# The first layer of a two-layer block, with its output products in three f32r terms and its order of work rewritten

## The reference

```
xn  = layernorm(x)
h   = rms_norm(xn) * norm_w
gate, hs = gelu(h @ fc_gate_w.T + b), h @ fc_w.T + b
r, i     = sigmoid(h @ fc_r_w.T + b), sigmoid(h @ fc_i_w.T + b)
a   = exp(-8 * softplus(alpha) * r)
s   = sqrt(1 - a*a) * hs * i
o_t = a_t * o_(t-1) + s_t                     # along each sequence
hs2 = o * gate + xn
h2  = rms_norm(hs2) * norm2_w
attn = ((h2 @ mlp_fc_w.T + b) * gelu(h2 @ mlp_gate_w.T + b)) @ out_w.T + out_b + hs2
ffn  = bitlinear(relu(bitlinear(xn, w_fc) + gate * (xn @ v.T @ fast_b.T @ u.T))**2, w_proj)
x1   = x + attn + ffn
```

## Time and profile before

| what | value |
|---|---|
| median of 3 runs | 2537.9 us (2536.19 to 2542.38) |
| span of the profiled execution | 2537.0 us |
| its own time apart from the span | not listed |
| PE busy over the span | 84% (weight loads 61%) |
| DVE, ACT, POOL busy over the span | 77%, 54%, 52% |
| granted TensorE clock, mean | 0.961 |

### The profile page before, as it was taken

How to read it: one execution, slowest core, us unless ns; L and a number is a source line. 1 busy time by engine, 2 the same in 40 slices (tenths; PEclk the granted TensorE clock), 3 DMA queues, 4 the chain that set the end, 5 groups by cost and what they waited for, 6 DMA issues and landing times. The chain is left out here.

```text
span 2537.0 us, 35012 instructions
## 1 busy us (share of the span) xinstructions
PE 2135.7 (84%) x10706; PEld 1539.2 (61%) x10706; DVE 1956.4 (77%) x2684; ACT 1376.4 (54%) x2333; POOL 1328.8 (52%) x953
## 2 busy tenths in 40 slices
PE   2699999999975788788878887867599999999995
PEld 1578777787751334333334333323399999999995
DVE  6644565545645999989898999899688888888883
ACT  1322233222326676667666666653277777777672
POOL 1112221122206999898989899997213333334433
PEclk8899999999987999999999999999899999999998
DMA  8010111101122213232223232314166667667663
GB/s 267 17 42 0 41 41 41 41 0 41 41 68 89 105 69 109 75 105 77 100 77 103 75 105 75 115 57 165 59 240 227 206 228 235 208 222 236 212 216 88
DMA packets 108971, 286.66 MB, mean 113 GB/s; under 512 B 20550, under 2 KB 85462, under 8 KB 90022
## 3 DMA queue, kind: packets, MB, share of 16 engines
q1 hardware_dynamic: 94598, 267.12, 30.1%
q0 software_dynamic: 14304, 18.75, 3.6%
HBM read 239.21 MB, written 50.82 MB: 114 GB/s over the span
## 5 line engine op out<-in xcount | busy, mean ns | idle before, releaser
L1103 POOL TENSOR_TENSOR m_work<-m_ux,m_bb 128x1024 f32<-128x1024 f32 x256 | 598.5, 2358 | 24.7 <-DVE m_hh L1387 22.1
L1251 ACT ACTIVATE m_da<-m_dl,m_A 128x512 f32<-128x512 f32 x512 | 349.3, 687 | 279.6 <-DVE m_hh L1387 278.8
L1486 PE MATMUL m_y<-m_work,m_ident 128*128 128x512 f32 x1024 | 493.0, 604 | 1.5 <-DVE m_work L1395 1.5
L1806 PE MATMUL e_h<-e_xTh,e_w1h 128*128 128x256 f32 x1248 | 353.4, 283 | 7.2 <-DVE e_xTl L1742 6.5
L1395 DVE TENSOR_TENSOR m_work<-m_hh,m_cb 128x1024 f32<-128x1024 f32 x256 | 312.7, 1222 | 48.8 <-PE m_cb L1460 25.6
L1806 PE MATMUL e_h<-e_xTl,e_w1h 128*128 128x256 f32 x1248 | 349.4, 280 | 0.0
L1806 PE MATMUL e_h<-e_xTh,e_w1l 128*128 128x256 f32 x1248 | 349.3, 280 | 0.0
L1387 DVE TENSOR_TENSOR_SCAN m_hh<-m_da,m_carry,m_work 128x512 f32<-128x512 f32 x256 | 313.9, 1268 | 7.4 <-POOL m_work L1103 7.3
L1387 DVE TENSOR_TENSOR_SCAN m_hh<-m_da,m_work 128x512 f32<-128x512 f32 x256 | 298.3, 1208 | 13.4 <-POOL m_work L1103 13.4
L1486 PEld LDWEIGHTS m_y<-m_work,m_ident 128*128 128x128 f32 x1024 | 198.3, 194 | 161.0 <-issue 147.9
L281 POOL TENSOR_TENSOR small<-mv,eps_ln 128x4 f32<-128x4 f32 x17 | 3.4, 201 | 551.3 <-DVE mv L399 551.3
(11 more groups left out here) (275 smaller groups left out, 4801.0 us busy)
## 6 DMA issues: line engine op xcount, KB each, us to landing
m_bb<-scratch_bT SPq DMA_DIRECT2D x64, 1024.0 KB
m_first<-in_w SPq DMA_DIRECT2D x20, 2048.0 KB, 7.5
e_w<-in_w SPq DMA_DIRECT2D x19, 2048.0 KB, 7.4
m_first<-in_w SPq DMA_DIRECT2D x20, 1024.0 KB, 10.1
e_w<-in_w SPq DMA_DIRECT2D x19, 1024.0 KB, 10.0
scratch_rec<-x1p SPq DMA_DIRECT2D x39, 260.0 KB, 8.3
e_xg<-scratch_rec SPq DMA_DIRECT2D x39, 260.0 KB, 2.8
e_b<-in_b SPq DMA_DIRECT2D x39, 128.0 KB, 3.0
```

What stands on the lines that cost most here:

```text
L1103: pool.tensor_tensor(bx[:, u % NB], ux[q % 2][:, cols], slot.to_broadcast([P, HALF, T]), ALU.mult).then_inc(s_bx, 1)
L1251: act.activation(da[d % NA][:], dl[q % 2][:, e], ACT.Exp, scale=A[:, at:at + 1]).then_inc(s_exp, 1)
L1486: last = mm(y[:, i], ident[:], hc[:, u % 4, i], start=False, stop=(n % NST == NST - 1))
L1806: last = mm(hbank[m % HR][:, j], w[i][:, k, cols], x[i][:, k], start=(p == 0 and k == 0 and j == 0), stop=(p == 2 and k == KD - 1 and j == 1),
```

## The change

Everything is in `layer0`, and the layouts in memory and the order of all engines are rewritten with it.

- **Output products.** w_o and w_j are split too. The outputs of the two feed-forward paths become 14 blocks of 512 tokens, each split into act_h and act_l (four buffers each). A block is multiplied as soon as it is there, in three f32r terms, into two banks of their own (`sums`), which gather all blocks of a chunk; six banks are left for the circular order. ACT makes ReLU and then the square twice (act_f in fp32, act_h in f32r) for an F block, and copies act_h for an MLP block; POOL subtracts for the F blocks, DVE for the MLP blocks.
- **Order.** These block products stand between the feed-forward and MLP products, two or three products after their own. The turns and logits of the chunk before stand there as well, MS moves behind F4, the gates of the next chunk end the chunk, and there is no ninth.
- **Preparation.** Loads have semaphores of their own and another order; each split and the turns and gates of chunk 0 wait for their own inputs; the ternary weights are made in a few passes over whole matrices.
- The loops are written out for the eight chunks on every engine.

The diff, cut to its core (functions that only get an index c more are left out):

```diff
+    RB = BANKS - 2
+    DEPTH = 4
+    NBLK = KH + KM
+    turns = ["XT0", "XT1", "HT0", "HT1"]
+    gates = ["R0", "R1", "I0", "I1", "H0", "H1", "GA0", "GA1"]
+    sides = ["N0", "N1", "Q0", "Q1"]
+    order = [(g, 0) for g in turns + gates]
+    for c in range(NCH):
+        order += [(f"F{m}", c) for m in range(3)]
+        order += [(g, c - 1) for g in sides if c > 0]
+        order += [("F3", c), ("F4", c), ("MS", c), ("F5", c)]
+        order += [("L", c - 1)] if c > 0 else []
+        order += [("F6", c), ("F7", c)]
+        order += [(f"{g}{m}", c) for m in range(KM) for g in ("MG", "MF")]
+        order += [(g, c + 1) for g in turns + gates if c + 1 < NCH]
+    order += [(g, NCH - 1) for g in sides + ["L"]]
+    place = {key: (k % RB, k // RB) for k, key in enumerate(order)}
...
+        sums = ctx.enter_context(nc.psum_tensor("sums", [P, 2, T], F32))
+
...
+        w_pl, w_ml, w_fl, w_ol, w_jl = (sb(f"w_{n}l", shapes[n], F32R) for n in "pmfoj")
+        act_h, act_l = (sb(n, [P, DEPTH, T], F32R) for n in ("act_h", "act_l"))
+        w_ph, w_mh, w_fh, w_oh, w_jh = (sb(f"w_{n}h", shapes[n], F32R) for n in "pmfoj")
...
+            sp_.dma_start(raw_p[:], dram["w_p"]).then_inc(wp_in, 16)
+            sp_.dma_start(vec[:], dram["vec0"]).then_inc(vec_in, 16)
+            sp_.dma_start(raw_f[:], dram["w_f"]).then_inc(wf_in, 16)
...
+            sp_.dma_start(raw_j[:], dram["w_j"]).then_inc(wj_in, 16)
+            sp_.dma_start(raw_m[:], dram["w_m"]).then_inc(wm_in, 16)
+            sp_.dma_start(raw_o[:], dram["w_o"]).then_inc(wo_in, 16)
...
+            sp_.dma_start(xres[:], rows(dram["x"], 0)).then_inc(xres_in, 16)
+            sp_.wait_ge(s_ln, 8)
+            sp_.dma_start(xt[:], rows(dram["x"], 1)).then_inc(x_in, 16)
...
+            def low_blocks(c):
+                for b in range(KH):
+                    pool.wait_ge(s_f, c * KH + b + 1)
+                    pool.wait_ge(s_hi, c * NBLK + b + 1)
+                    block_free(pool, c, b)
+                    pool.tensor_tensor(act_l[:, b % DEPTH], act_f[:, b % 2], f32(act_h[:, b % DEPTH]),
+                                       ALU.subtract).then_inc(s_lf, 1)
+
+            next_scales(0)
+            pool.wait_ge(act_prep, ap["wmh"])
+            pool.tensor_tensor(w_ml[:], raw_m[:], f32(w_mh[:]), ALU.subtract).then_inc(s_wml, 1)
+            pool.wait_ge(act_prep, ap["woh"])
+            pool.tensor_tensor(w_ol[:], raw_o[:], f32(w_oh[:]), ALU.subtract).then_inc(s_wol, 1)
+            for c in range(NCH):
+                if c > 0:
+                    out_scales(c - 1)
+                low_blocks(c)
                 pool.wait_ge(xres_in, c * 16 + 16)
...
                 pool.tensor_tensor(xres[:], xres[:], brow[:].rearrange("p (o d) -> p o d", o=1).to_broadcast([P, SUB, D]),
                                    ALU.add).then_inc(s_xb, 1)
-                pool.wait_ge(s_st1, c * 9 + 9)
-                row_scales(small1, mv1, s_pw1, c * 7, eps_rms1)
+                if c + 1 < NCH:
+                    next_scales(c + 1)
+            out_scales(NCH - 1)
...
+            act.wait_ge(wf_in, 16)
+            act.activation(abs_f[:], raw_f[:], ACT.Abs).then_inc(act_prep, 1)
+            act.wait_ge(dve_prep, dp["norm_p1"])
+            act.activation(w_ph[:], raw_p[:], ACT.Copy).then_inc(act_prep, 1)
...
+            def relu_squares(ms, c):
                 for m in ms:
                     wait_filled(act, f"F{m}", c)
-                    inc_drained(act.activation(fT[:, m], ps(f"F{m}")[:], ACT.Relu), f"F{m}")
-
...
+                    inc_drained(act.activation(act_r[:, m % 2], ps(f"F{m}", c)[:], ACT.Relu), f"F{m}", c)
+                    wait_drained(act, f"F{m}", c)
+                    if m >= 2:
+                        low_done(act, c, m - 2)
+                    elif c > 0:
+                        low_done(act, c - 1, NBLK - 2 + m)
+                    act.activation(act_f[:, m % 2], act_r[:, m % 2], ACT.Square).then_inc(s_f, 1)
+                    block_free(act, c, m)
+                    act.activation(act_h[:, m % DEPTH], act_r[:, m % 2], ACT.Square).then_inc(s_hi, 1)
...
+            def high_mid(m, c):
+                b = KH + m
+                wait_drained(act, f"MF{m}", c)
+                block_free(act, c, b)
+                act.activation(act_h[:, b % DEPTH], act_f[:, b % 2], ACT.Copy).then_inc(s_hi, 1)
...
+            act.activation(sgn_f[:], raw_f[:], ACT.Sign).then_inc(act_prep, 1)
+            turned_x(0)
+            act.activation(w_mh[:], raw_m[:], ACT.Copy).then_inc(act_prep, 1)
+            gate("R", aT, "r_b", ACT.Sigmoid, 0)
+            act.wait_ge(wj_in, 16)
+            act.activation(abs_j, raw_j[:], ACT.Abs).then_inc(act_prep, 1)
+            gate("I", iT, "i_b", ACT.Sigmoid, 0)
+            act.activation(sgn_j, raw_j[:], ACT.Sign).then_inc(act_prep, 1)
+            act.wait_ge(dve_prep, dp["ca"])
+            decay(0)
+            act.wait_ge(wo_in, 16)
+            act.activation(w_oh[:], raw_o[:], ACT.Copy).then_inc(act_prep, 1)
+            act.wait_ge(dve_prep, dp["low1"])
+            act.activation(w_fh[:], raw_f[:], ACT.Copy).then_inc(act_prep, 1)
+            root(0)
+            gate("GA", gT, "gate_b", ACT.Gelu, 0)
+            act.wait_ge(dve_prep, dp["tern_j"])
+            act.activation(w_jh[:], raw_j[:], ACT.Copy).then_inc(act_prep, 1)
+            for c in range(NCH):
+                if c > 0:
+                    turned_x(c)
+                    gate("R", aT, "r_b", ACT.Sigmoid, c)
+                    gate("I", iT, "i_b", ACT.Sigmoid, c)
+                    decay(c)
+                    root(c)
+                    gate("GA", gT, "gate_b", ACT.Gelu, c)
+                elif c == 0:
+                    act.wait_ge(dve_prep, dp["wfl"])
+                relu_squares(range(3), c)
...
+            def low_mid(m, c):
+                b = KH + m
+                dve.wait_ge(s_hi, c * NBLK + b + 1)
+                dve.tensor_tensor(act_l[:, b % DEPTH], act_f[:, b % 2], f32(act_h[:, b % DEPTH]),
+                                  ALU.subtract).then_inc(s_lm, 1)
...
+            dve.wait_ge(act_prep, ap["sgn_f"])
+            dve.tensor_tensor(abs_f[:], abs_f[:], over(half_f, KD), ALU.subtract).then_inc(dve_prep, 1)
+            dve.tensor_tensor(sgn_f[:], sgn_f[:], over(scale_f, KD), ALU.mult).then_inc(dve_prep, 1)
+            dve.wait_ge(dve_prep, dp["mul_f"])
+            dve.scalar_tensor_tensor(out=raw_f[:], in0=abs_f[:], scalar=0.0, in1=sgn_f[:], op0=ALU.is_gt,
+                                     op1=ALU.mult).then_inc(dve_prep, 1)
...
+            for k in range(KD):
+                dve.wait_ge(p_low, k + 1)
+                dve.tensor_tensor(raw_f[:, k], raw_f[:, k], sums[:].rearrange("p a t -> p (a t)"),
+                                  ALU.add).then_inc(dve_prep, 1)
+            sum_x(0)
+            dve.wait_ge(act_prep, ap["wfh"])
+            dve.tensor_tensor(w_fl[:], raw_f[:], f32(w_fh[:]), ALU.subtract).then_inc(dve_prep, 1)
+            dve.wait_ge(dve_prep, dp["half_j"])
+            dve.wait_ge(act_prep, ap["sgn_j"])
+            dve.tensor_tensor(abs_j, abs_j, over(half_j, KH), ALU.subtract).then_inc(dve_prep, 1)
+            dve.tensor_tensor(sgn_j, sgn_j, over(scale_j, KH), ALU.mult).then_inc(dve_prep, 1)
+            dve.wait_ge(dve_prep, dp["mul_j"])
+            dve.scalar_tensor_tensor(out=raw_j[:], in0=abs_j, scalar=0.0, in1=sgn_j, op0=ALU.is_gt,
+                                     op1=ALU.mult).then_inc(dve_prep, 1)
+            dve.wait_ge(act_prep, ap["wjh"])
+            dve.tensor_tensor(w_jl[:], raw_j[:], f32(w_jh[:]), ALU.subtract).then_inc(dve_prep, 1)
+            for c in range(NCH):
+                if c > 0:
+                    turned_h(c)
+                    turned_x(c)
+                    out_rows(c - 1)
+                    sum_x(c)
+                    squares(c)
+                    gated_input(c)
+                    out_normed(c - 1)
+                recur(c)
+                if c > 0:
+                    out_sum(c - 1)
+                    turned_n(c - 1)
...
+            def into_sums(b, c):
+
+                low_done(pe, c, b)
...
+                wh, wl = (w_jh[:, b], w_jl[:, b]) if b < KH else (w_oh[:, b - KH], w_ol[:, b - KH])
+                for s in range(SUB):
+                    cols = slice(s * P, (s + 1) * P)
+                    out = sums[:, s // 2, s % 2 * D:(s % 2 + 1) * D]
+                    for p, (a, w) in enumerate(((act_h, wh), (act_h, wl), (act_l, wh))):
+                        last = mm(out, a[:, b % DEPTH, cols], w, start=(b == 0 and s % 2 == 0 and p == 0),
+                                  stop=(b == NBLK - 1 and s % 2 == 1 and p == 2), skip_group_check=True)
+                last.then_inc(s_blk, 1)
...
+            pe.wait_ge(act_prep, ap["wfh"])
+            pe.wait_ge(dve_prep, dp["wfl"])
+            for c in range(NCH):
+                feed(0, c)
+                feed(1, c)
+                feed(2, c)
```

(89 more changed lines are left out.)

670 lines of the change are left out of this document (310 added, 360 removed).

## The result

The changed kernel takes **2459.8 us** (median of four runs, 2458.2 to 2460.9) against 2538.3 for the kernel before (four runs, 2536.2 to 2542.4): a ratio of 0.9688, with a 95% interval of 0.9674 to 0.9702. The profiled execution has a span of 2457.1. The forecast was 2458, with a range of 2420 to 2496. The number came out; several of the steps under it did not, and their errors cancelled by luck.

A forecast was written before the change was run, and what follows sets the result against it. TensorE was taken to bound each chunk, and the preparation the first 79 us. Preparation -28.6, seven periods -35.4 and the end -14.8 sum to -78.8 against 2537: 2458 us, range 2420 to 2496.

The forecast's parts named there:

- Nothing later changes: Stages after the first layer: claimed to keep their times, so the first layer's 78.8 us gain is the whole gain.
- The period: First layer, one 512-token chunk in steady state: from 80.05 to 75.0 us, 35.4 less over seven periods.
- Block 0's wait: First output block of each chunk: TensorE waits about 2.4 us for POOL's subtraction.
- the wait at the mean square: Mean-square product of each chunk: TensorE waits 2.1 us for VectorE's first copy of turned rows to free the bank.
- The recurrence has three POOL turns in it: VectorE's recurrence in each chunk: three POOL subtractions take turns with it, so it ends near 25.5 us into the chunk.
- Rival (a): Loop and preparation: DVE and POOL do not hinder each other; period 71.3, preparation 68, total 2421 us; chance 0.21.
- The preparation: First layer, start to chunk 0's mean-square product: 75 us against 103.59, a gain of 28.6.
- The end: First layer, last chunk's mean-square product to last logits: 56.6 us in place of 71.4, a gain of 14.8.
- (b): Loop: POOL comes last behind DVE's back-to-back work, block 0 starts at 24 us, 4.7 more a chunk: 2496 us; chance 0.11.
- (c): Loop gains nothing because ACT's chain through two squares paces the blocks; only the preparation gains: 2509 us; chance 0.05.
- (d): Loop: waits drop TensorE's clock to 1.2 GHz through the feed-forward half; 91 us a chunk, about 2586 us; chance 0.04.
- (e): Output products: f32r terms run at 0.28 us each, not 0.113, 47 against 23.4 a chunk: 2682 us; chance 0.01.

The follow-up runs named there:

- e8: The changed kernel without POOL's eight low subtractions per chunk (the third term of those blocks reads the high part again): 2436.6 us.
- e10: The changed kernel with one fp32 matmul in place of the three f32r terms of each output block: 2495.5 us.
- e9: The changed kernel without POOL's two subtractions for the low parts of the middle and output weights (products read the high part twice): 2448.6 us.
- e7: The changed kernel with only one of the three f32r terms of every output block (112 matmuls less a chunk): 2430.2 us.

## Why the prediction was right, and where it was not

**The total** was right by 2 us, and that is luck: a gain that was put 20.7 too small (78.8 against 99.5) met a loss of 20.8 that was not foreseen.

**"Nothing later changes"** is the step that failed. It rested on unchanged code. The rows were read in that very stage, but for what two engines do to each other, not for the ring that they stand in: it took nearly TensorE's 17.17 us, and nothing in the sum asked how much room there was. The view to ask was the waits of POOL and SP in that stage: SP waited for the shares before its loads of rows, so its queue ran at the ring's pace already:

```profile
SPq L1626 <- POOL e_share L1607: 423.7, 35, 13.2
```

**The period**, 75.0 against 71.27. TensorE's own work was right: 67.9 forecast; at full clock 70.69 less the 3.06 of that period's wait is 67.6. Block 0's wait was right in place, releaser and size (2.4; 17.3 / 7 = 2.5). It is 3.06 or 2.03 in turn, from chunk to chunk; first a chunk with the long wait, then one with the short:

```profile
352.96 5.68 POOL L326 TENSOR_TENSOR act_l<-act_f,act_h 128x512 fp32r<-128x512 f32 x3 [6.07 <-ACT act_h L395]
...
355.30 0.39 PE L789 MATMUL sums<-w_jh,act_h 128*128 128x256 f32 x1 [3.06 <-POOL act_l L326]
...
351.86 2.33 DVE L559 TENSOR_TENSOR_SCAN qT<-aT,iT 128x512 f32<-128x512 f32 x2
354.41 3.09 DVE L569 TENSOR_TENSOR qT<-qT,gT 128x512 f32<-128x512 f32 x2
...
357.43 2.36 DVE L573 TENSOR_TENSOR hs<-qT,hs 128x512 f32<-128x512 f32 x2
```

```profile
282.35 1.27 POOL L326 TENSOR_TENSOR act_l<-act_f,act_h 128x512 fp32r<-128x512 f32 x1 [6.07 <-ACT act_h L395]
...
281.25 3.45 DVE L559 TENSOR_TENSOR_SCAN qT<-aT,carry,iT 128x512 f32<-128x512 f32 x2
```

The terms that were too large are the wait at the mean square (2.1; 2.1 us over all seven periods, 0.3 each), h2's 0.4 and the first gate's 0.5 (none seen), and the clock (1.6; 1.0 by the periods told of at e8). That is 3.3 of the 3.7; the 0.3 that TensorE's own work came out lower is most of the rest.

"The recurrence has three POOL turns in it" is borne out. In the chunk with the long wait POOL's first subtraction is held by the scan (2.29 where others take 1.27), and the three then hold three of VectorE's products: 3.09 and 2.36 for pairs that take 1.3 each in e8, 2.9 us in all. In the chunk with the short wait they hold the second scan (3.45 for the pair, 2.5 in e8) and two products. What was too large around them is the length of VectorE's chain: counted from the first gate product of the chunk (337.10 in the first of the two), the recurrence ends at 23.9 and not at 25.5, and the first copy of the turned rows at 25.8 and not at 28.4, while TensorE comes to the mean square at 27.1 and not at 26.3. So nothing is left to wait for.

Rival (a) priced a period without any turn-taking at 71.3, which is what came, but not for its reason: the turns are there. With POOL's subtractions gone the period is 67.9 (e8), so they cost 3.35 a chunk. Not all of that is turn-taking, which the forecast put at 3.7 (75.0 less 71.3). An estimate from these waits: 1.4 is POOL's own subtraction ahead of block 0 (a wait of 2.03 where its first is not held, 0.7 without it), 0.4 that the scan holds it in three chunks of seven, 0.3 the mean square and 1.0 the clock.

**The f32r terms**: 4.4 forecast, 3.7 measured (e10).

**The preparation**, 75 against 79.81. The steps came as forecast up to the gated input (45; 44.9). Then two terms were short. The additions of the low rank were given 5 us and took 8.4 (44.93 to 53.28), with TensorE's small products between them:

```profile
43.43 3.75 PE L852 MATMUL sums<-mg,low_z 16*128 16x512 f32 x4 [6.98 <-DVE sq L644]
49.96 2.06 PE L852 MATMUL sums<-mg,low_z 16*128 16x512 f32 x4
```

From the low half of `w_j` to the mark 10 were given and 11.3 passed. The two waits for POOL's splits were seen in advance and were worth 7.4 (e9).

**The end**: 56.6 forecast, 57.2 measured. One subtraction in the forecast is off: 19.7 less 3.0 and 2.7 leaves 14.0 and not 13.3, which would have given 57.3.

**The rivals.** (b) and (c) fall with the period. (d) falls in its size, not in its kind: the loop's granted clock is 0.95 to 1.00, but with TensorE waiting some 8 us a chunk it is 0.91 to 0.96 (e7). With the rule of the Trainium skill ("TensorE: Matmul & The Clock Gate", section "HAM oscillation — how this bites in real kernels"), kernels that start every pass slow after a wait, the preparation agrees (0.83); the steady loop, whose waits reach 3.06 us, keeps 0.95 to 1.00. (e) falls: terms follow each other by 0.11 to 0.12 (355.53, 355.64, 355.77). ScalarE's three table loads ahead of block 0 take 1.28 each with the next activation right behind (346.13, then 347.42), so the 4.1 us more that were weighed for them did not come.

## What to carry to other kernels

An engine that is busy all the time can hide a ring of transfers that takes just as long as it does; before writing "nothing later changes", add up that ring, and ask what half a microsecond more would do to it (here 192 KB more to load, an estimated 0.6 us, cost 18 us over the stage). Where two engines take turns, a wait that is covered comes back at the next place in the order, so look up what stands right ahead of the release, and move that too. A wait of TensorE costs its own length and, in some periods, a lower clock for the work behind it.

## What the runs showed that was not expected

Unchanged code lost 20.8 us behind a change 1100 us earlier; what in that change made its loads slower stays open. 192 KB more per tile cost 18 us with two buffers for the row numbers and the shares (1 KB each), and nothing with four. An instruction of VectorE that takes 0.69 us took 5.64 beside one of POOL. And a kernel with 112 matmuls less in a chunk (12.7 us of TensorE's time) gained 4.2.
